# Mamba-style mixer and top-2 experts on one core: low parts split before a VectorE transposition, and one more wait in TensorE's stream

## The reference

```
xn  = layernorm(x)
xp, z = split(xn @ w_in)                 # 256 -> 2 x 512
xc  = silu(causal_conv4(xp) + conv_b)    # per channel, 4 taps
h_t = 0.9 h_(t-1) + 0.1 (xc_t @ w_B)     # state of 16, a scan over tokens
x1  = x + ((h @ w_C) * silu(z)) @ w_out
idx = top2(layernorm(x1)[token 0] @ Wr + br)
out = x1 + 1/2 sum over e in idx of (gelu(layernorm(x1) @ W1[e] + b1[e]) @ W2[e] + b2[e])
```

## Time and profile before

| what | value |
|---|---|
| median of 3 runs | 506.76 us (506.46 to 507.39) |
| profiled execution, its own time | 505.8 us |
| its span, first to last instruction | 504.0 us |
| TensorE busy | 498.7 us, 99% of the span |
| VectorE, ScalarE, GpSimd busy | 90%, 79%, 69% |
| granted TensorE clock, mean | 0.999 of 2.4 GHz |

### The profile page before, as it was taken

How to read it: one execution, slowest core, us unless ns; L and a number is a source line. 1 busy time by engine, 2 the same in 40 slices (tenths; PEclk the granted TensorE clock), 3 DMA queues, 4 the chain that set the end, 5 groups by cost and what they waited for, 6 DMA issues and landing times.

```text
span 504.0 us, 9945 instructions
## 1 busy us (share of the span) xinstructions
PE 498.7 (99%) x3026; PEld 440.4 (87%) x3026; DVE 452.9 (90%) x896; ACT 400.2 (79%) x692; POOL 348.7 (69%) x390
## 2 busy tenths in 40 slices
PE   8999999999999999999999999999999999999997
PEld 7888799788888988888888888988889888888997
DVE  6999999989998899989999899998999989996773
ACT  4986959878869788697887969779797888969554
POOL 4959597559693696928969197782977649764291
PEclk9999999999999999999999999999999999999999
DMA  8940105344151532605235160432604333130102
GB/s 259 298 179 6 37 1 179 114 142 153 64 190 42 167 125 83 208 10 199 82 125 166 42 221 28 165 126 83 208 31 136 125 126 126 47 120 1 42 2 85
DMA packets 53380, 57.29 MB, mean 114 GB/s; under 512 B 8682, under 2 KB 49642, under 8 KB 53226
## 3 DMA queue, kind: packets, MB, share of 16 engines
q1 hardware_dynamic: 51498, 56.67, 33.7%
q10 hardware_dynamic: 1856, 0.31, 0.3%
HBM read 35.46 MB, written 21.50 MB: 113 GB/s over the span
## 4 chain that ended last, share of the span: by engine, by line
PE 98%; DVE 1%; DMA 1%; issue 0%; DVEq 0%
PE blk L1299 16%; PE blk L1302 16%; PE blk L1308 16%; PE tok L1422 12%; PE tok L1424 12%; PE tok L1423 11%; PE blk L1510 3%; PE turn L1489 3%; PE turn L1486 3%; PE turn L1246 1%; PE tok L1308 1%; PE tok L1302 1%; PE tok L1299 1%; DMA x_mid<-in_L_attn_x 1%; DVE stats_t L917 0%; DVE normed L934 0%
## 5 line engine op out<-in xcount | busy, mean ns | idle before, releaser
L992 DVE SCALAR_TENSOR_TENSOR conv<-blk,tap_w,conv 128x512 f32<-128x512 f32 x192 | 130.1, 742 | 7.2 <-ACT conv L683 6.3
L488 POOL TENSOR_TENSOR y_lo<-gate,y_hi 128x512 fp32r<-128x512 f32 x57 | 72.2, 1297 | 35.9 <-ACT y_hi L611 35.8
L1299 PE MATMUL blk<-xn_hi,w_in_hi 128*128 128x512 f32 x228 | 89.6, 393 | 0.0
L1302 PE MATMUL blk<-xn_hi,w_in_lo 128*128 128x512 f32 x228 | 89.0, 390 | 0.0
L453 POOL TENSOR_TENSOR xc_lo<-conv,xc_hi 128x512 fp32r<-128x512 f32 x60 | 73.2, 1236 | 7.5 <-ACT xc_hi L611 7.4
L1422 PE MATMUL tok<-w_out_hi,y_hi 128*128 128x256 f32 x256 | 71.1, 278 | 0.0
L1423 PE MATMUL tok<-w_out_lo,y_hi 128*128 128x256 f32 x256 | 70.8, 276 | 0.0
L1424 PE MATMUL tok<-w_out_hi,y_lo 128*128 128x256 f32 x256 | 70.7, 276 | 0.0
L1308 PE MATMUL blk<-xn_lo,w_in_hi 128*128 128x512 f32 x228 | 70.4, 390 | 0.0
L1422 PE MATMUL tok<-w_hi,hid_hi 128*128 128x256 f32 x248 | 69.8, 281 | 0.2
L1424 PE MATMUL tok<-w_hi,hid_lo 128*128 128x256 f32 x248 | 69.3, 279 | 0.0
(11 more groups left out here) (189 smaller groups left out, 1320.5 us busy)
## 6 DMA issues: line engine op xcount, KB each, us to landing
spill<-normed SPq DMA_DIRECT2D x25, 512.0 KB, 2.9
normed<-spill SPq DMA_DIRECT2D x100, 128.0 KB, 2.8
out<-x_mid SPq DMA_DIRECT2D x30, 256.0 KB, 2.4
x_mid<-in_L_attn_x SPq DMA_DIRECT2D x29, 256.0 KB, 2.8
x_in<-in_L_attn_x SPq DMA_DIRECT2D x14, 512.0 KB, 3.8
w_all<-in_L_ffn_W SPq DMA_DIRECT2D x2, 2048.0 KB, 11.3
b_all<-in_L_ffn_b SPq DMA_DIRECT2D x1, 1024.0 KB, 13.9
gate<-in_L_attn_w_in SPq DMA_DIRECT2D x2, 256.0 KB, 4.8
```

The lines of the kernel that those rows point to most:

```text
L488: nc.gpsimd.tensor_tensor(y_lo[:, j, :], gate_of(o, j), y_hi[:, j, :].bitcast(F32), ALU.subtract).then_inc(y_lo_set, 1)
L992: nc.vector.scalar_tensor_tensor(cols, blk[j][:], tap_w[:, j, t:t + 1], cols, ALU.mult, ALU.add).then_inc(tap_added, 1)
L1299: ins = mm(dst, whi(k), his(k), start=(k == 0), stop=False)
L1302: mm(dst, wlo(k), his(k), start=False, stop=False)
```

## The change

In VectorE's stream, `hidden_lo` is moved ahead of `turn_squares`, in even and odd steps. In TensorE's stream, the loop's last twelve down products get a `behind_next` of their own: it waits for `c_ready`, which each product of `state_out` increments, at the value that the first of the four gives, with a register `c_nth` that grows by four (JD) a step.

```
@@ VectorE, step, q == 0
                         moments1(a + 2)
+                    hidden_lo(f, range(JF))
                     if has_next(s, 1):
                         turn_squares(a + 1)
-                    hidden_lo(f, range(JF))
                     if has_attn(s):
                         scan(a, 0)
@@ TensorE
+            c_nth = nc.tensor.alloc_register("c_nth")
+            nc.tensor.reg_mov(c_nth, FIRST * JD + 1)
...
-            def behind_next(tail, nth):
+            def behind_next(tail, nth, step=1):
                 pe.sem_inc(paced, 1)
                 pe.wait_ge(tail, nth)
                 for _ in range(PACE - 1):
                     pe.sem_inc(paced, 1)
-                nc.tensor.reg_add(nth, nth, 1)
+                nc.tensor.reg_add(nth, nth, step)
...
                     turns2(LAST - 1)
+                if not isinstance(a, int):
+                    behind_next(c_ready, c_nth, JD)
                 down(f, 1, (2, 3))
```

## The result

| | before | after |
|---|---|---|
| median, runs side by side | 506.77 us (506.46 to 507.39, 4 runs) | 513.24 us (512.81 to 513.34, 4 runs) |
| ratio, 95% interval | | 1.0124 (1.0107 to 1.0142) |
| profiled execution, its span | 505.8, 504.0 us | 512.81, 511.0 us |

The change made the kernel 6.5 us slower; 513.2 was forecast.

A forecast was written before the change was run, and what follows sets the result against it. TensorE was taken as the bound, with VectorE's chain to `state_out` just behind. Delays 5.66 + `xp` 0.36 + lead 0.5 - pace 0.1 = +6.4 us, on 506.8 giving 513.2 us; 8-in-10 range 510.5 to 516.0.

The forecast's parts named there:

- The bound: Whole kernel: TensorE is 98% of the chain, with VectorE's chain to `state_out` just behind it.
- Odd steps: Steps 5, 7, 9, 11, 13: TensorE waits 0.37 us each for the state at `state_out`, 1.85 us in all.
- The scan's +1.80: VectorE: the scan starts 1.80 us after the last `hid_hi` ends, through wait 0.03, low part 0.61, transposition 1.16.
- least effective distance: From the end of the state's low part to a full-speed `state_out`: 0.14 us, 0.09 plus 0.05 lost inside.
- Even steps: Steps 6, 8, 10, 12 and written-out 14: TensorE waits 0.65 us each at `state_out`, 3.25 us in all.
- the fourth low part can't start before the fourth `hid_hi` has ended: VectorE's `hidden_lo`: coming earlier gains nothing, so the 1.16 us transposition stands uncovered between last low part and scan.
- "half" rival: A shorter scan-to-state chain, `state_lo` at 0.69 not 1.03 us: 5 x 0.34 less, 511.5 us; no chance given.
- Steps 3 and 4: `state_out` comes 0.28 us later in step 4; step 3 gets the same price, 0.56 us for both.
- `xp` at 5.56 us: Behind four more even steps, `xp` waits for `ys` and takes 5.56 instead of 5.47 us: 0.36 us in all.
- The lead of the sequencer: TensorE's sequencer, at 0.07 us a product, loses its lead at the loop's branch: 0.5 us for all five passes.
- the rival of a dearly lost lead: Every pass pays 1.1 us at the branch, not the first alone: 5.5 instead of 0.5, 518.2 us; chance 0.1.
- The quicker pace: Last twelve `down` products at 113 instead of 118 ns behind an emptying wait: 0.1 us gained, odd steps only.

The follow-up runs named there:

- e4: Kernel before with hidden_lo ahead of the transposition in even steps only, without the wait on c_ready: 508.19 us, ratio 1.0040.
- e9: Kernel after with GpSimd's two bias operations (b_sum, b_sel) left out in the loop's even steps: 510.73 us, ratio 1.0081 against the kernel before.
- e1: Kernel after without its wait on c_ready, so only VectorE's new order remains: 512.89 us, ratio 1.0127 against the kernel before.
- e7: Kernel before with three low parts ahead of the transposition and the fourth behind it: 512.23 us, ratio 1.0107.
- e12: Kernel before with three low parts, transposition, fourth low part, and GpSimd's two bias operations left out in the loop's even steps: 508.92 us, ratio 1.0048.
- e2: Kernel before with only the wait on c_ready and its register added, VectorE's order unchanged: 506.07 us, ratio 0.9994.
- e8: Kernel before with the wait on c_ready set to the last of state_out's four products instead of the first: 512.28 us, ratio 1.0107.

## Why the prediction was right, and where its terms were off

- **The bound** was read rightly. TensorE stops for nothing new but the state's low part, and the new waits stand there and nowhere else.
- **Odd steps**, 0.37 us each: measured 4.50 + 1.03 - 5.17 = 0.36 to 0.38 in all five. The scan's +1.80, the unchanged chain from the scan to the low part, and the least effective distance (0.05 from the low part's end to `state_out`, and 0.11 lost inside its four products, 0.16 against the forecast's 0.14) all came as worked out.
- **Even steps**, 0.65 us each: the sum's mis-sized term. In the four steps 6 to 12 they cost 0.89 to 1.03. For step 8: the forecast's 0.80 + 0.14 - 0.29; measured, the scan came 0.59 us later than +1.80, the state's low part took 0.34 less, 0.65 + 0.59 - 0.34 = 0.90. The step that failed is "the fourth low part can't start before the fourth `hid_hi` has ended, and that is tied to `up` on TensorE": true, but in even steps what the fourth one waited for was the third, 0.62 us longer than for its `hid_hi`. Two things together do it. VectorE comes 0.6 us later into `hidden_lo`, measured against the last `hid_hi`; e4, with the odd steps left alone, has it back in time. And two of the low parts run beside GpSimd's `b_sum` and `b_sel`; e9 takes these away and the 0.59 us with them, at the same lateness. Either alone moves the scan by nothing: in e4 the low parts take 3.23 us beside GpSimd and the scan still starts at +1.82.
- The Trainium skill, "SBUF — State Buffer", section "Who interferes with whom", says that a VectorE instruction with two inputs in SBUF contends with a GpSimd instruction that reads SBUF, and one with a single input doesn't (outside its two-port modes). The rows agree: `hidden_lo` with two inputs takes 3.24 against 2.63 us for four, the transposition with one takes 1.23 us on either side. By that rule the exchange moves an operation that GpSimd can't disturb out of GpSimd's way and puts one there that it can; the forecast did not use it.
- **How long the contention lasts** can be read from the state's low parts of all kernels here. Where an instruction of GpSimd's addition (L498) is still running when the low part starts, the low part takes 0.69 us and what is left of that instruction less 0.14 us, and never under 0.69: with 0.04, 0.15, 0.39, 0.47 and 0.63 us left it takes 0.69, 0.70, 0.94, 1.02 and 1.18. So it looks like a wait for one instruction's end and not like a slower pace. No run here took the addition away, so this is read from the rows alone.
- **The "half" rival's mechanism**, the state's low part at 0.69 us instead of 1.03, did come true: over all 15 of the span the state's low parts take 690 ns in the mean, 819 before. The delay moves them behind GpSimd's addition (L498 ends at 259.74 in step 8 of the kernel after, the low part starts at 259.68; before, it ran on to 257.45, and the low part started at 255.83). The rival was priced at -1.7 us; it was hidden under the 5 x 0.59 = 2.9 us of the contended, late low parts of the five even loop steps.
- **Steps 3 and 4**, 0.28 each: 0.45 and 0.82 from `down` on. The forecast had counted from the last `hid_hi`, and so counted `state_out` is 0.18 and 0.52 us later, with the 0.11 lost inside its four products; the rest is that `down` starts earlier. Step 4's low parts are late and contended like those of other even steps (the scan at +2.40).
- **`xp` at 5.56 us**, +0.36: didn't come. The low parts behind the state (`turn1_lo`) take 1.29 us instead of 1.72, so `ys` starts 261.61 - 260.37 = 1.24 us after the state's low part ends, not the 1.67 of the earlier trace rows, and `xp` at 262.82 doesn't meet it. The neighbour from which this was priced, step 6, had the slow low parts.
- **The lead of the sequencer**, +0.5: didn't come. The lines of TensorE's sequencer in step 9 of the kernel after (count, durations in ns, first and last start; L1439 is the wait, L1440 the register addition, L265 the branch back):

```profile
L1439 PEldq EVENT_SEMAPHORE  x2: 51/51/51, 291.5 to 291.7; - x2
...
L1440 PEldq ALU_OP  x1: 32/32/32, 291.8 to 291.8; - x1
...
L265 PEldq ALU_OP  x1: 32/32/32, 292.0 to 292.0; - x1
...
L265 PEldq FUSED_REGOPS  x1: 41/41/41, 292.3 to 292.3; - x1
```

It passes the twelve products between 291.8 and 292.0 and is back at the loop's head at 292.3, when the array has just begun them (the first at 292.01, the last at 293.26). The forecast's 0.07 us a product, from the earlier trace rows, was no rate of the sequencer: on the way from 282.8 to 285.4 it also had to wait for the last low part, which ends at 283.17 + 0.69 = 283.86, and 18 of the 36 products are issued behind it. What held it after that isn't shown. The first passage, 1.5 us in the kernel before, takes 0.4 us here (from 168.6 to 168.9). With it the rival of a dearly lost lead falls: `score` and `xp` follow without a gap in all passes.
- **The quicker pace**, -0.1: -0.42 in the trace, since it came in even steps too (where `xp` didn't wait for `ys`), and in step 3 and 14, which have no wait. e1 shows that the order's stalls bring it alone. The forecast's reading that the quicker pace stands right behind a wait goes too far: the first 36 of `down` have a wait ahead of them and go at 118 ns in seven of the ten loop steps of the kernel before.
- **The sum** came so close by luck, since these errors mostly cancel: +1.7 in the steps, -0.4 for `xp`, -0.5 for the lead and the rest, -0.3 for the pace, +0.6 in all (before rounding) on the profiled executions (7.0, not 6.4). That the medians lie only 6.5 apart took this away too: the kernel after was profiled 0.43 us under its median, the one before 0.96. Without the two terms that never came the forecast would have been 0.9 us lower, 512.3.

Open: why VectorE comes earlier or later into an even step was followed only as far as the odd step before it. In e7 and e12 the odd steps cost nothing, and VectorE still came 2.05 us ahead in even steps and not 2.56. That the branch costs nothing in the first pass was seen in the trace and not tested by itself. Nor does any run say what gives a group of products the quicker or the slower pace. No version beat the kernel before by more than can be measured; the wait alone (e2) is the only one that may gain.

## What to carry to other kernels

An operation that costs nothing where it stands is covered by something: before moving it, look at what its old place was beside, on the other engines too, and which instruction will stand there in its stead. An engine that comes 2.5 us ahead of a deadline may come 0.6 us later after a delay of its own in the step before, as VectorE did here, so price a reorder over two consecutive steps, and not one by one. A price taken from a neighbouring step carries that step's contention with it; take the row's uncontended length as well, and keep both ends.

## What the runs showed of the hardware

- Two VectorE operations of one shape take different times by what GpSimd does beside them: four low parts 128x512 take 2.63 us alone and 3.24 us beside two GpSimd operations of 128x256; the state's low part (64x512) takes 0.69 us alone and up to 1.18 when an instruction of GpSimd's addition is running as it starts. The transposition of 128x1024 stays at 1.21 to 1.24.
- A wait on TensorE's sequencer for the first of four products cost nothing (e2); for the last of them 0.60 us (e8), and the array stood empty in between.
- Twelve products of 256 columns take 1.36 or 1.41 us in most steps, and 1.37 to 1.40 or 1.43 in some. The first is frequent behind a wait or a stall, but not certain: the first 36, which have a wait ahead of them in every kernel here, take anything from 4.08 to 4.32 us in steps where `state_out` doesn't wait. Behind the full stop of e8 the twelve take 1.45, and the first of them shows 0.36 us instead of 0.28.
- TensorE's sequencer passed twelve products with their weight loads in about 0.2 us (291.8 to 292.0 in step 9 of the kernel after), where at most three products were still ahead of it.
